# Causal attention of a four-layer kernel: the four value blocks of a head group multiplied in one visit, a second buffer for the first block's exponentials

## The reference

```python
def heads(W):
    return (x @ W).reshape(B, S, NUM_HEADS, D_K).transpose(0, 2, 1, 3)
Q, K, V = (heads(WQ), heads(WK), heads(WV))
score = jnp.einsum('bhqd,bhkd->bhqk', Q, K) / jnp.sqrt(D_K)
score = score + mask                     # -inf above the diagonal
score = score - jnp.max(score, axis=-1, keepdims=True)
score = jnp.exp(score)
score = score / jnp.sum(score, axis=-1, keepdims=True)
out = jnp.einsum('bhqk,bhkd->bhqd', score, V)
return out.transpose(0, 2, 1, 3).reshape(B, S, E) @ WO
```

## Time and profile before

| | |
|---|---|
| time, median of 3 runs | 659.02 us |
| the profiled execution: span from first to last instruction | 654.6 us |
| difference, outside the span | 4.4 us |
| TensorE busy | 583.0 us (89%) |
| VectorE busy | 402.2 us (61%) |
| ScalarE busy | 316.2 us (48%) |
| GpSimd busy | 172.9 us (26%) |
| row units on TensorE (L1615) | 160 of 452 ns mean |
| values on TensorE (L1643) | 512 instructions of 442 ns mean, overlapping |
| maxima on VectorE (L1052) | 160 of 681 ns mean |

### The profile page before, as it was taken

How to read it: one execution, slowest core, us unless ns; L and a number is a source line. 1 busy time by engine, 2 the same in 40 slices (tenths; PEclk the granted TensorE clock), 3 DMA queues, 4 the chain that set the end, 5 groups by cost and what they waited for, 6 DMA issues and landing times.

```text
span 654.6 us, 9264 instructions
## 1 busy us (share of the span) xinstructions
PE 583.0 (89%) x3347; PEld 433.0 (66%) x3347; DVE 402.2 (61%) x958; ACT 316.2 (48%) x543; POOL 172.9 (26%) x185
## 2 busy tenths in 40 slices
PE   8889989999998379999649698899999999998997
PEld 3556556556564258787536476688778878786866
DVE  6778788798884511432248986884669556762430
ACT  4756566556665204534216243752575255643351
POOL 6112122452543630000058623611300041001100
PEclk9999999999999579999969798999999999999999
DMA  4773242243110455834111100100000000000000
GB/s 130 223 247 110 77 130 65 82 145 97 55 44 2 137 167 167 263 90 118 41 32 32 30 4 2 34 0 1 1 17 2 1 0 18 1 0 1 18 1 17
DMA packets 44926, 42.51 MB, mean 65 GB/s; under 512 B 4176, under 2 KB 34384, under 8 KB 44880
## 3 DMA queue, kind: packets, MB, share of 16 engines
q1 hardware_dynamic: 42544, 37.44, 18.8%
q0 software_dynamic: 2048, 4.20, 2.2%
q10 hardware_dynamic: 288, 0.28, 0.2%
HBM read 25.12 MB, written 16.78 MB: 64 GB/s over the span
## 4 chain that ended last, share of the span: by engine, by line
PE 66%; DVE 10%; ACT 7%; issue 6%; DMA 5%; POOL 4%; SPq 2%; DVEq 0%; POOLq 0%; ACTq 0%
PE ps L1945 7%; PE ps L1615 6%; PE ps L1898 5%; PE ps L1631 5%; PE ps L1643 5%; PE ps L1967 5%; PE ps L1968 4%; PE ps L1889 4%; PE ps L2048 4%; PE ps L2044 4%; PE ps L2045 4%; PE ps L1971 4%; PE ps L1961 2%; DMA XS<-xs_dram 2%; PE ps L1618 2%
## 5 line engine op out<-in xcount | busy, mean ns | idle before, releaser
L679 ACT ACTIVATE PT<-ps 128x384 f32<-128x384 f32 (+1 forms) x192 | 93.5, 529 | 69.9 <-PE ps L1631 67.5
L1052 DVE TENSOR_REDUCE pm<-ps 128x4 f32<-128x512 f32 x160 | 102.3, 681 | 10.0 <-PE ps L1615 9.4
L1615 PE MATMUL ps<-KP,QS 128*128 128x512 f32 x160 | 71.7, 452 | 7.9 <-DVEq L1045 2.5
L546 POOL TENSOR_SCALAR_AFFINE_SELECT PT<-PT 128x512 f32<-128x512 f32 x64 | 39.9, 636 | 129.1 <-ACT PT L679 129.1
L1631 PE MATMUL ps<-QM,KP 128*128 128x512 f32 (+3 forms) x256 | 69.1, 331 | 1.5 <-DVE QM L1066 1.1
L1631 PEld LDWEIGHTS ps<-QM,KP 128*128 128x128 f32 x256 | 43.8, 189 | 22.8 <-issue 12.6
L796 ACT ACTIVATE HT<-ps,cols 128x640 f32<-128x640 f32 x32 | 25.4, 795 | 54.8 <-PE ps L1889 54.8
L1615 PEld LDWEIGHTS ps<-KP,QS 128*128 128x128 f32 x160 | 29.8, 188 | 27.5 <-DVE pm L1052 11.5
L1414 DVE TENSOR_TENSOR_SCAN zero<-decay,OG 128x512 f32<-128x512 f32 x32 | 44.8, 1400 | 1.1
L1643 PE MATMUL ps<-PT,V 128*32 128x128 f32 (+3 forms) x512 | 44.6, 442 | 0.0
L521 POOL TENSOR_TENSOR rstd<-veps,mhalf 128x4 f32<-128x4 f32 x11 | 12.7, 1157 | 110.7 <-DVE veps L963 110.5
(11 more groups left out here) (300 smaller groups left out, 1309.2 us busy)
## 6 DMA issues: line engine op xcount, KB each, us to landing
qk_dram<-HL SPq DMA_DIRECT2D x24, 256.0 KB, 3.5
W<-in_eW SPq DMA_DIRECT2D x16, 256.0 KB, 3.6
QS<-qk_dram SPq DMA_DIRECT2D x15, 256.0 KB
KP<-qk_dram SPq DMA_DIRECT2D x60, 64.0 KB, 2.4
xs_dram<-zero SPq DMA_DIRECT2D x4, 640.0 KB, 3.5
XS<-xs_dram SPq DMA_DIRECT2D x8, 320.0 KB, 5.0
ys_dram<-zero SPq DMA_DIRECT2D x8, 320.0 KB, 2.9
whole_h_w<-in_h_w SPq DMA_DIRECT2D x2, 1024.0 KB, 9.7
```

The source lines that it names most:

```text
L546: g.affine_select(out=diag, in_=diag, pattern=[[0, 4], [1, P]], compare_op=ALU.is_ge, fill=0.0, base=0, channel_multiplier=-1).then_inc(se ...
L679: act.activation(PT[:, i, a:z], bank[ROWB + n % KEYB][:, 0:z - a], ACT.Exp, scale=float(DK) ** -0.5).then_inc(exp_done, 1)
L1052: v.tensor_reduce(pm[:, t, k, :], bank[n % ROWB].rearrange("p (i n) -> p i n", n=P), AXX, ALU.max).then_inc(row_free[n % ROWB], 1)
L1615: mm = pe.matmul(to, QS[:, G % 2, t * P:(t + 1) * P], KP[:, G % 3, k, :, :].rearrange("p i n -> p (i n)"), start=True, stop=t != k)
```

## The change

- The three places of `values` become one: all four blocks of group w - 1 stand in group w behind key unit 3. Only in the last group, which has no row units of a next group, `values(w, 0)` stays where it was, and its blocks 1 to 3 follow as before.
- The exponentials of the first key block get a buffer of their own, `PT0`, twice, used in turn by even and odd groups; exponential 0 of group w waits for the values of group w - 2. The buffer lies where later stages keep weights.
- `round_halves(b + 1)` on ScalarE stands ahead of exponential 6 and no longer behind exponential 7.
- `row_max(w + 1, 8)` on VectorE stands ahead of `normalise(w - 1)`.

```diff
@@ -204,11 +204,15 @@
+        with ExitStack() as beside:
+            PT0 = beside.enter_context(nc.sbuf_tensor("PT0", [P, 2, 4, SEQ], F32, side="right"))
...
-            PT = early("PT", [P, 4, PTW])
+            PT = early("PT", [P, 4, PTW - SEQ])
@@ -350,6 +354,12 @@
+        def weights_of(w, i, a, z):
+
+            if z <= SEQ:
+                return PT0[:, w % 2, i, a:z]
+            return PT[:, i, a - SEQ:z - SEQ]
@@ -673,10 +683,11 @@
-                if i == 0 and w:
-                    act.wait_ge(pv_done, TB * (w - 1) + js[-1] + 1)
+                back = 2 if c == 0 else 1
+                if i == 0 and w >= back:
+                    act.wait_ge(pv_done, TB * (w - back) + js[-1] + 1)
@@ -751,10 +762,10 @@
                 exp_unit(w, 4)
                 exp_unit(w, 5)
+                if g == 0 and b + 1 < NB:
+                    round_halves(b + 1)
                 exp_unit(w, 6)
                 exp_unit(w, 7)
-                if g == 0 and b + 1 < NB:
-                    round_halves(b + 1)
@@ -1179,10 +1190,10 @@
                     row_max(w + 1, 7)
+                    row_max(w + 1, 8)
                 if w:
                     normalise(w - 1)
                 if rows_next:
-                    row_max(w + 1, 8)
                     row_max(w + 1, 9)
@@ -1745,7 +1756,6 @@
                     key_scores(w - 1, 11)
-                    values(w - 1, 1)
@@ -1765,8 +1775,8 @@
                 key_scores(w, 3)
                 if w:
-                    values(w - 1, 2)
-                    values(w - 1, 3)
+                    for j in range(TB):
+                        values(w - 1, j)
@@ -1779,7 +1789,8 @@
                     project(b + 1)
-                values(w, 0)
+                if not rows_next:
+                    values(w, 0)
                 key_scores(w, 6)
```

More of the change, by code:

```diff
@@ L544, in select @@
                 for j in KC[c]:
-                    diag = PT[:, :, OFF[j]:OFF[j] + P]
+                    diag = weights_of(w, slice(0, 4), OFF[j], OFF[j] + P)
                     g.affine_select(out=diag, in_=diag, pattern=[[0, 4], [1, P]], compare_op=ALU.is_ge, fill=0.0, base=0,
@@ L675, in exp_unit @@
                 a, z = OFF[js[0]], OFF[js[-1] + 1]
-                if i == 0 and w:
-                    act.wait_ge(pv_done, TB * (w - 1) + js[-1] + 1)
+                back = 2 if c == 0 else 1
+                if i == 0 and w >= back:
+                    act.wait_ge(pv_done, TB * (w - back) + js[-1] + 1)
                 act.wait_ge(ts_full, NKU * w + n + 1)
-                act.activation(PT[:, i, a:z], bank[ROWB + n % KEYB][:, 0:z - a], ACT.Exp,
+                act.activation(weights_of(w, i, a, z), bank[ROWB + n % KEYB][:, 0:z - a], ACT.Exp,
                                scale=float(DK) ** -0.5).then_inc(exp_done, 1)
@@ L1643, in values @@
                     mm = pe.matmul(bank[6][32 * i:32 * i + 32, j * P:SEQ], V[:, j * H + g * 4 + i, :],
-                                   PT[:, i, OFF[j]:OFF[j + 1]], start=(j == 0), stop=(j == TB - 1),
+                                   weights_of(w, i, OFF[j], OFF[j + 1]), start=(j == 0), stop=(j == TB - 1),
                                    skip_group_check=True)
```

## The result

The kernel after takes 667.57 us (median of 4 runs, 666.6 to 667.66) against 658.59 us (median of 4) for the kernel before, run beside it: 1.0159 times as long, 95% interval 1.0139 to 1.0178. The change costs 9.0 us. The forecast was 3.65, so the sign was right and the size far too small. The profiled execution goes from a span of 654.6 to 664.8 us, 10.2 more, and those 10.2 us are what the traces let one divide.

A forecast was written before the change was run, and what follows sets the result against it. TensorE bounds plain groups before; after, VectorE starves behind the long visit. Plain groups 0.6, sequence 1 0.18, sequence 2 0.92, sequence 3 0.65 and last group 1.3 sum to +3.65 us on 659.0: 662.7 us, range 658.3 to 665.8.

The forecast's parts named there:

- the visit's start and length: Values behind key unit 3: the four-block visit starts 3.47 us behind `add_max` and takes 2.28 us.
- the halves' wait: Groups g = 0 with projection: VectorE's 2.54 us wait for `round_halves`, behind exponential 7 and block 0, goes.
- three plain groups: Sequence 0's groups, bound by TensorE: 10.20 us against 10.00 each, as the saving is lost waiting for VectorE.
- last group, to S: From the last `add_max` to the first scatter (S): the visit holds up ScalarE's sums, +1.3 us.
- g = 1: Second group of a sequence: the product with WO ends earlier and VectorE bounds, 12.15 us against 12.85.
- g = 0: First group of a sequence, with projection: ScalarE's queue comes last, 12.60 us against 13.62 in sequence 1.
- 0.72 until `MX` is written: Last piece of VectorE's tail in a group, read from the earlier trace, within a tail of 3.24 us.
- the bounds: Allowances around the sum: earlier visit -7 us, free long visit -1.5, useless halves +1.6, a further first-unit wait +2.8.
- the kept visits (1): Rival: TensorE stays the bound and 0.68 us is saved in 14 groups, 648 us; chance 0.04.
- the earlier visit (2): Rival: key unit 0 and row unit 4 don't wait, so 7 us come back, 655.7 us; chance 0.11.
- the draw (3): Rival: 3.5 us come back, gains in g = 0 and g = 1 balance other losses, 659.2 us; chance 0.12.
- Rival 4: The halves don't help as exponentials 6 to 9 come late, 1.6 us gone, 664.3 us; chance 0.08.

The follow-up runs named there:

- e9: e3 with the load of a later layer's weights (layer 1's Wo, 512 KB) moved later: 664.32 us, 1.0101 times the kernel before.
- e10: e9 plus eight spare products nobody reads, ahead of the last group's key unit 0: 663.35 us, 1.0105 times the kernel before.
- e3: The changed kernel with GpSimd's `select(w, 1)` held until the next group's `MX` is written: 665.35 us, 1.0121 times the kernel before.
- e4: The changed kernel with spare products, two ahead of each `turn_max`, eight ahead of the last group's key unit 0: 669.43 us, 1.0186 times the kernel before.
- e1: The kernel before with only `round_halves` moved ahead of exponential 6: 656.98 us, 0.9993 times the kernel before.
- e11: The changed kernel with values blocks 0 and 1 behind key unit 11, 2 and 3 behind key unit 3, second selection held: 655.92 us, ratio 0.9981 to before.
- e2: The kernel before with only the single visit of values and the second buffer: 675.87 us, 1.0296 times the kernel before.

## Why the prediction was right in sign and wrong in size

The mechanism held point by point: the visit's start and length, VectorE idle ahead of row 7's maximum (1.95 us, released by L1626; "nearly 2 us" was said), TensorE then waiting for `MX` ahead of L1668, the halves' wait gone. The groups, against what e9 and e10 measure at full clock and without the collision:

| | before | forecast | after | without both (e9, e10) |
|---|---|---|---|---|
| three plain groups | 30.00 | +0.6 | +1.61 | +0.74 |
| sequence 1 | 48.79 | +0.18 | +0.25 | -0.27 |
| sequence 2 | 48.05 | +0.92 | +2.58 | +0.50 |
| sequence 3, three groups | 33.80 | +0.65 | +1.32 | +1.05 |
| last group, to S | 10.07 | +1.3 | +3.03 | +1.40 |
| sum | | +3.65 | +8.79 | +3.42 |

So the sum of the forecast, 3.65, is right for the terms it has: 3.42, pieced together from groups of two runs. With all of sequence 3 taken from e10 it is 3.38. Inside it g = 1 (12.06 for 12.15) and w = 12 (10.69 for 10.60) were near, g = 0 was 0.2 better (12.41 for 12.60) and w = 14 some 0.35 worse (12.03 to 12.08 for 11.70). The other 1.4 us of the 10.2 are: start and group 0, -0.14; scatters to expert 0, +0.07; expert 0 to the gathers, +1.47; the rest, +0.04.

The failure is what the sum lacked, 8.79 - 3.42 = 5.4 us in the attention and 1.5 at expert 0:

1. *The tail.* "0.72 until `MX` is written" was taken over unchanged from the earlier trace rows. It became 61.37 - 60.38 = 0.99, because the two engines' order in time changed: `select(w, 1)` follows exponentials on ScalarE, and `MX` was now later than it. In the table it is 0.87 in the plain groups, 0.52 and 0.27 in sequences 1 and 3, and about 0.5 in sequence 2: some 2.2 us. e3 shows it by removing it: it takes back 0.85 us in the plain groups and 0.48 in sequence 1, where neither run has a fall of the clock.
2. *The clock.* 13.99 - 12.39 = 1.6 us in group 8, 13.10 - 11.47 = 1.6 in the last, and the 1.5 at expert 0, with 6.26 against 4.65 us in its first product. The forecast wrote that "What follows [...] moves with it", at full speed, and the bounds had no term for the clock. For the last group e4 and e10 show the cause, the wait ahead of key unit 0; for the other two the half clock is read from the trace, and what brought it is not shown.

Of the rivals, the kept visits (1), the earlier visit (2) and the draw (3) are out by the visit's start at 3.46 and by plain groups above 10.00. Rival 4 is out by e1 and the 12.41. Rival 5's 666 us was near the time for another reason: the row units wait 3.4 us in all for KP's loads, where it was 1.9, but all of it in the first group, and start and group 0 together take no longer. Part of the difference lies in the baseline. The working took the 4.4 us between the median, 659.02, and the profiled span, 654.6, for time outside the span. Runs that list both have 1.7 to 1.8 us there (666.6 for a span of 664.8, 659.0 for 657.3). So the profiled execution of before was a fast one, near 656.4 us, and this is why the traces differ by 10.2 us and the medians by 9.0.

Saying 662.7 with an upper end of 665.8 was too narrow, since the bounds were made only of what the sum already held.

## What to carry to other kernels

When an edit makes one engine later by a fraction of a microsecond, look at what other engines start within that fraction, and not only at what waits by semaphore: here a `tensor_scalar` of 0.18 us slid under a GpSimd instruction and took 0.47, and the profile showed it only as a longer duration, with no wait. Ask of any work that is gathered in one place which engine loses the cover that the scattered pieces gave: the same blocks in one visit cost 9 us and in two visits at another place nothing. And where an edit gives TensorE a longer wait, bound the price of a slower clock behind it by the half-clock rows that the trace has.

## What the runs showed of the hardware

- A VectorE `tensor_scalar` on 128 x 16 took 0.18 us alone and 0.45 to 0.64 where it started early in GpSimd's affine select, ending with it; held apart, 0.18 to 0.19 in all 16 groups (e3, e9, e10, e11). A reduction (L1069) that ran wholly inside the select took its usual 0.26 us (e2, at 60.72).
- The half clock came in short stretches in the attention, which cost from 0.5 us (group 1 of e10, 10.77 for 10.24) to 2.6 us (last group of e9, 14.11 for e10's 11.47), and moved between groups from kernel to kernel.
- A stage that no edit touched took 84.5 to 84.7 us in some profiled runs and 86.1 to 87.5 in others. That is as much as most edits here are worth, so gains were judged at `add_max` of the last group and by the medians, and both are given.
- In three runs, all of one chip, ScalarE and VectorE started about 1 us behind what they waited for in group 8, and TensorE stood 1.0 us (e2, e3, e4); e4 has it in group 12 too. No row names a cause.
